# Q and K stacks written by DMAs inside SBUF instead of selection matmuls, in a gated cross-attention and mixture-of-experts block

## The reference

```python
x = x + tanh(g_xattn) * cross_attention(layernorm(x), ctx)   # softmax over 512 context rows
X = layernorm(x); h = rmsnorm(X) * norm1_w
q, k, v = h @ wq, h @ wk, h @ wv                             # 16 heads of 8
X = X + concat_heads(softmax(q k^T * 8**-0.5) v) @ wo        # 256 x 256 scores a head
h2 = rmsnorm(X) * norm2_w
combine = softmax weights of the top 2 of 8 experts (softmax(h2 @ router_w))
moe = swiglu_shared(h2) + sum_e combine[e] * swiglu_e(h2)    # inner width 256
x = x + tanh(g_ffn) * (X + moe)
```

## Time and profile before

| | us |
|---|---|
| median of three runs | 265.34 (265.28 to 267.71) |
| profiled execution | 265.57 |
| its span, first to last instruction | 263.8 |
| PE busy | 220.2 |
| DVE busy | 155.4 |
| ACT busy | 134.0 |
| POOL busy | 50.6 |

### The profile page before, as it was taken

One profiled execution on the slowest core, in us unless ns is written; L12 is line 12 of the kernel. 1 busy time (PEld: TensorE's weight loads), 2 busy tenths in 40 slices (PEclk: granted clock), 3 DMA queues, 4 the chain that ended last, 5 costly groups with the idle time before them and its releaser, 6 DMA issues.

```text
span 263.8 us, 4600 instructions
## 1 busy us (share of the span) xinstructions
PE 220.2 (83%) x1671; PEld 187.5 (71%) x1671; DVE 155.4 (59%) x397; ACT 134.0 (51%) x249; POOL 50.6 (19%) x81
## 2 busy tenths in 40 slices
PE   7791677787867788799979859999999959999995
PEld 6461556465756556577676639888899949999995
DVE  2658515880776935357438796663556565555554
ACT  2942364415286678698868744555424732222220
POOL 6609301154210700001810530011002000000000
PEclk9998668986799999999999998999999989999999
DMA  5900000002020210000330000000000000000000
GB/s 135 278 3 0 1 2 0 0 0 65 0 60 0 66 56 1 2 0 2 82 98 2 0 2 0 0 2 4 1 22 0 0 2 20 2 1 21 1 2 20
DMA packets 5174, 6.32 MB, mean 24 GB/s; under 512 B 448, under 2 KB 3392, under 8 KB 5152
## 3 DMA queue, kind: packets, MB, share of 16 engines
q1 hardware_dynamic: 5152, 6.02, 8.3%
HBM read 5.50 MB, written 0.52 MB: 23 GB/s over the span
## 4 chain that ended last, share of the span: by engine, by line
PE 58%; ACT 16%; DVE 15%; issue 6%; POOL 4%; DVEq 0%; ACTq 0%; POOLq 0%
PE bank L1051 11%; PE bank L1040 6%; PE bank L1039 6%; PE bank L1041 6%; PE bank L1022 5%; PE bank L1007 4%; ACT k_st L501 4%; PE bank L930 3%; PE bank L996 3%; DVE mxs L782 3%; ACT k_st L438 2%; ACT ep L548 2%; PE bank L1060 2%; PE bank L867 2%; PE bank L891 2%
## 5 line engine op out<-in xcount | busy, mean ns | idle before, releaser
L782 DVE TENSOR_REDUCE mxs<-bank 128x2 f32<-128x512 f32 x64 | 43.1, 689 | 20.4 <-PE bank L996 19.6
L548 ACT ACTIVATE ep<-bank 128x512 f32<-128x512 f32 x64 | 37.6, 599 | 19.3 <-PE bank L1007 18.2
L1039 PE MATMUL bank<-h2hi,whi 128*128 128x256 f32 x144 | 44.0, 306 | 0.0
L1051 PE MATMUL bank<-down_s,early 128*128 128x128 f32 x288 | 39.3, 280 | 3.4 <-DVE early L802 3.3
L1040 PE MATMUL bank<-h2lo,whi 128*128 128x256 f32 x144 | 41.4, 288 | 0.0
L1041 PE MATMUL bank<-h2hi,wlo 128*128 128x256 f32 x144 | 41.0, 285 | 0.0
L1051 PEld LDWEIGHTS bank<-down_s,early 128*128 128x128 f32 x288 | 36.1, 196 | 4.0 <-DVE early L802 4.0
L996 PE MATMUL bank<-k_st,q_st 96*128 96x256 f32 x128 | 30.8, 322 | 6.5 <-DVE mxs L782 3.8
L568 ACT ACTIVATE early<-bank 128x512 f32<-128x512 f32 x28 | 16.6, 597 | 38.2 <-PE bank L1041 38.2
L802 DVE TENSOR_TENSOR early<-early,bank 128x512 f32<-128x512 f32 x28 | 19.2, 687 | 27.9 <-PE bank L1041 21.4
L1007 PE MATMUL bank<-q_st,k_st 96*128 96x256 f32 x128 | 28.5, 304 | 2.7 <-ACT k_st L501 1.2
(11 more groups left out here) (146 smaller groups left out, 341.9 us busy)
## 6 DMA issues: line engine op xcount, KB each, us to landing
raw<-expert_w SPq DMA_DIRECT2D x9, 256.0 KB, 2.8
down_s<-expert_w SPq DMA_DIRECT2D x9, 128.0 KB, 2.7
early<-ctx_T SPq DMA_DIRECT2D x1, 672.0 KB, 9.3
xs<-x_tiles SPq DMA_DIRECT2D x2, 256.0 KB, 5.1
out_dram<-x SPq DMA_DIRECT2D x4, 128.0 KB, 2.0
ffn_s<-ffn_w SPq DMA_DIRECT2D x1, 261.0 KB, 9.3
attn_s<-attn_w SPq DMA_DIRECT2D x1, 242.0 KB, 2.8
early<-ctx_T SPq DMA_DIRECT2D x1, 224.0 KB, 6.4
```

The source lines that it names most:

```text
L548: nc.scalar.activation(ep[:, n % NEP].rearrange("p t s -> p (t s)"), b_of(("exp", n))[:], ACT.Exp, scale=SCALE_H).then_inc(free(("exp", n) ...
L782: nc.vector.tensor_reduce(mxs[:, half % 2, :, 64 + h:65 + h], b_of(("max", n))[:].rearrange("p (t s) -> p t s", t=TB), AX_X, ALU.max).then ...
L1039: pe.matmul(bank, whi[:, fs], h2hi[:, hs], start=True, stop=False)
L1051: last = pe.matmul(b_of(("down", n))[:, j * D:(j + 1) * D], act_t[:, n % 2, f * L + j * P:f * L + (j + 1) * P], down_s[:, f, e * D:(e + 1) ...
```

## The change

The stacks are written by DMAs from `split` to `q_st` and `k_st`, with no matmul or cast. `wq` and `wk` are reordered on the host (`by_parity`), so that one parity's heads are 64 neighbouring partitions; each DMA takes 64 partitions of 1 KB and writes eight partitions of 8 KB, 16 DMAs a sequence. SP issues them, but eight of sequence 0's are issued by ScalarE behind its `qk_split`. There are three stack buffers. Pads of buffer 0 are cleared by GpSimd early (step z), its picks are copied by ACT, and SP copies both to buffers 1 and 2 by eight DMAs (`copy_pads`). Rows beyond 64 are 16 instead of 32. For sequence 3, which takes buffer 0 again, GpSimd clears the maxima rows (step c3). Step t is GpSimd's clearing of `mxs` and `vh`, steps m its expert splits, now tied to the slots. `u`, `h2T`, `h2hi` and `h2lo` share memory with tiles that are no longer in use. Banks are given by kind from sets (`BANKS`), the one unused for longest first. All items up to the last slot use tanh.

```diff
-NSTACK = 2
+NSTACK = 3
-FIRST_STEPS = """f0 g0 xn0 f1 q0 g1 s0 xn1 s1 p0 q1 o0 p1 s2 o1 f2 s3 n0 p2 g2 h0 o2 xn2 p3 k0
-                 e0 q2 e1 o3 e2 w0 e3 n1""".split()
-MIXED_STEPS = {0: "s4 h1", 1: "f3", 2: "k1 s5", 3: "p4 g3", 4: "e4 xn3", 5: "o4 p5", 6: "e5 q3", 7: "o5 s6", 8: "e6 n2",
-               9: "p6 s7", 10: "e7 h2", 11: "o6", 12: "p7 k2", 13: "w1", 14: "o7", 16: "n3", 17: "e8", 19: "h3",
-               21: "e9 k3", 25: "e10", 29: "e11", 31: "w2", 33: "e12", 37: "e13", 41: "e14", 45: "e15", 47: "w3"}
+FIRST_STEPS = """f0 g0 xn0 f1 z0 q0 g1 s0 xn1 s1 p0 f2 q1 o0 p1 s2 g2 o1 s3 n0 p2 xn2 h0 o2 k0 p3 t0
+                 q2 o3 s4 n1 w0 f3 s5 h1 p4 k1""".split()
+MIXED_STEPS = {0: "g3 o4", 1: "p5 xn3", 2: "o5", 3: "q3 n2", 4: "s6", 5: "s7", 6: "h2", 7: "p6 w1", 8: "k2 o6 m0", 9: "p7",
+               10: "o7", 11: "n3 m1", 13: "h3", 15: "k3 m2 m3", 18: "m4", 27: "c3", 31: "w2", 42: "m5 m6 m7 m8", 47: "w3"}
+BANKS = {"turn": (0, 1, 6), "proj": (2, 3, 7), "sum": (4, 5), "misc": (4, 5)}
...
-    NSEL = 96
+    NSEL = 64 + NH
...
-    last_exp = NHEADS - 1 + LAG
+    last_exp = SLOTS_A
...
+        def stack(eng, b, heads):
+            s = b % NSTACK
+            eng.wait_ge(hi_ready, b + 1)
+            is_read(eng, ("qk2", b))
+            if b >= NSTACK:
+                is_full(eng, ("exp", NH * (b - NSTACK + 1) - 1))
+            for p in heads:
+                for a in range(2):
+                    for c in range(2):
+                        r = 32 * p + 16 * a + 8 * c
+                        for qk, part, stack in ((0, a, q_st[r:r + 8, s]), (1, c, k_st[r:r + 8, s, p * NG:(p + 1) * NG])):
+                            rows = split[64 * p:64 * p + 64, b % 2, part, qk, :].bitcast(F32)
+                            eng.dma_start(stack.bitcast(F32), rows).then_inc(stacked[b], 16)
+        def copy_pads(sp, s):
+            words, maxima = k_st[:].bitcast(F32), q_st[:].bitcast(F32)
+            sp.dma_start(words[0:32, s, NG:], words[0:32, 0, NG:]).then_inc(padded[s], 16)
+            sp.dma_start(words[32:64, s, :NG], words[32:64, 0, :NG]).then_inc(padded[s], 16)
+            sp.dma_start(words[64:NSEL, s], words[64:NSEL, 0]).then_inc(padded[s], 16)
+            sp.dma_start(maxima[64:NSEL, s], maxima[64:NSEL, 0]).then_inc(padded[s], 16)
...
-            for e in range(NEXP):
+            for e in range(NRAW):
+                load_expert(sp, e)
+            sp.wait_ge(picks_ready, 2)
+            sp.wait_ge(pads_ready, 1)
+            for b in range(1, NSTACK):
+                copy_pads(sp, b)
+            stack(sp, 0, (0,))
+            for b in range(1, NSTACK):
+                stack(sp, b, (0, 1))
+            for e in range(NRAW, 5):
+                load_expert(sp, e)
+            stack(sp, NSTACK, (0, 1))
+            for e in range(5, NEXP):
...
             def split_h2(b):
                 is_read(pool, ("h2T", b))
+                if b == 0:
+                    pool.wait_ge(stacked[2], 256)
+                    pool.wait_ge(stacked[3], 256)
...
                     qk_split(i)
                     if i == 0:
-                        copy_picks(1)
+                        stack(act, 0, (1,))
...
-                    if h % 4 == 0:
-                        written(("stq", n // 4))
-                        written(("stk", n // 4))
+                    if h == 0:
+                        if 1 <= b < NSTACK:
+                            pe.wait_ge(padded[b], 64)
+                        else:
+                            pe.wait_ge(pads_ready, b // NSTACK + 1)
+                        pe.wait_ge(stacked[b], 256)
```

More of the change, by code:

```diff
@@ L46, with bank_uses @@
 NRAW = 2
[L49 to L54, removed]
+def bank_uses(kinds, uses):
+    place, taken, count = {}, {}, {}
+    for n, (kind, use) in enumerate(uses):
+        bank = min(kinds[kind], key=lambda i: taken.get(i, i - 8))
+        place[use] = (bank, count.get(bank, 0))
+        taken[bank], count[bank] = n, count.get(bank, 0) + 1
     return place
@@ new lines, in _ @@
+            for stage, i in order:
+                if stage == "f":
+                    norm1(i)
+                elif stage == "g":
+                    if i == 0:
+                        pool.wait_ge(ld_attn, 16)
+                        pool.wait_ge(tg_ready, 1)
+                        step(nc.gpsimd.tensor_scalar(bv_row, bv_row, tg[:, 0:1], None, ALU.mult))
+                    add_bias(i)
+                elif stage == "o" and i % TB == TB - 1:
+                    norm2(i // TB)
+                elif stage == "z":
+                    pool.wait_ge(norm1_out, 2)
+                    pool.wait_ge(xb_ready, 1)
+                    clear_pads(i)
+                elif stage == "t":
+                    tables()
+                elif stage == "m":
+                    split_weights(i)
+                elif stage == "c":
+                    clear_maxima(i)
+                elif stage == "a":
+                    for kind, b in read_at.get(i, []):
+                        if kind == "square":
+                            norm3(b)
+                        if kind == "h2T":
+                            split_h2(b)
@@ L511, in misc @@
                     is_full(act, use)
-                    rows = b_of(use)[64:NSEL, 0:L].unsqueeze(1).broadcast_to([32, NG // 2, L])
+                    if b == 0 and half == 0:
+                        for i in range(1, NSTACK):
+                            act.wait_ge(padded[i], 64)
+                    rows = b_of(use)[64:NSEL, 0:L].unsqueeze(1).broadcast_to([NH, NG // 2, L])
                     nc.scalar.mul(q_st[64:NSEL, b % NSTACK, 4 * half:4 * half + 4, :], rows, -1.0).then_inc(free(use), 1)
@@ L833, in _ @@
                     qk_rest(i)
-                elif stage == "e" and i < 4:
-                    stack_out(i)
                 elif stage == "a":
@@ L918, in v2_proj @@
                 last.then_inc(full(("v2", b)), 1)
-            def make_stacks(i):
-                b, part = i // 4, i % 4
-                if i == 0:
-                    pe.wait_ge(sel_ready, 8)
-                pe.wait_ge(hi_ready, b + 1)
-                written(("qk2", b))
-                for qk, use, rows in ((0, ("stq", i), sel_q), (1, ("stk", i), sel_k)):
-                    may_fill(pe, use)
-                    for n in range(2):
-                        for hl in range(2):
-                            last = pe.matmul(b_of(use)[0:NSEL if qk == 0 else 64, n * L:(n + 1) * L],
-                                             rows[:, hl, 2 * part + n, :], split[:, b % 2, hl, qk, :],
-                                             start=(hl == 0), stop=(hl == 1))
-                    last.then_inc(full(use), 1)
             def misc(step, b):
@@ L1083, in _ @@
                     v2_proj(i)
-                elif stage == "e":
-                    make_stacks(i)
                 elif stage == "a":
```

153 lines of the change are left out of this document (43 added, 110 removed).

## The result

| | before | after |
|---|---|---|
| median us (runs) | 266.52 (4, same chip) | 247.30 (4; 245.17 to 248.91) |
| ratio, 95% interval | 1 | 0.925 [0.915, 0.935] |
| profiled execution, its span | 265.57, 263.8 | 245.17, 243.1 |

The account below looks back on a forecast made before the run. Steps waiting for each other at the start, no full engine, then PE with ACT, then DVE with PE, lastly PE bound it. Stages 45 + 31.5 + 36 + 24 + 99 = 235.5 us of span, forecast 237, range 222 to 256.

Parts of the forecast that it names:

- the forecast's own band of 230 to 245: Whole kernel: the time lands near the forecast of 237 us; chance 0.48.
- Slots 18 to 47: Third stage, stack groups between attention slots: their ACT and PE work goes, 36 us instead of 48.3, bounds 33 and 41.
- the rival of 252 (245 to 260): Between slots PE waits for DVE's maxima, not ACT's casts, so only PE's own share goes: 252 us; chance 0.25.
- The start: Everything ahead of slot 0: the later of ScalarE's path to k1 and the stack transfers, 45 us against 46.3, bounds 42 to 52.
- the narrow case: Stack transfers: eight of 64 written rows give an eighth of the ways, 1.87 us each, 30 us a sequence.
- Slots 0 to 17: Second stage: DVE's 26 us at its share of slots 48 to 63 give 31.5 us instead of 43.4, bounds 27 and 36.
- Transfers of sequences 1 to 3 hidden: Stack DMAs needed at slots 16, 32 and 48: at between 4 and 20 us a sequence no wait shows.
- The sign that I named: Stack DMAs: each lands under 10 us after its issue.
- the slower rival: Stack transfers become the bound, 30 us a sequence one after the other, slot 48 at 151, total 276 us; chance 0.07.
- Banks: PSUM: pv, down and small transposes share two banks instead of four; emptied in time, otherwise up to 12 us lost.
- Tail: Expert items behind slot 63: 99 us instead of 101.5, bounds 96 and 102; table loads cause part of five items' 5.9 lost.
- Expert loads and pad copies behind the stacks: SP's queue: expert loads behind stack DMAs have 16 slots of cover, and pad copies of 6.5 us run during the statistics.

Follow-up runs that it names:

- The copies and the matmuls put back: Two kernels: the changed kernel plus 24 ScalarE copies of 96x512, or plus eight more PE matmuls at each of eight slots from 17 to 45: 256.76 and 250.22 us.
- the y pairs free: Changed kernel with GpSimd waiting for DVE's norm pairs before clearing pads or tables and splitting experts 0 and 1: 236.51 us, 0.890 of before.
- the fastest kernel: Changed kernel with GpSimd waiting for DVE's norm pairs, stack rows four partitions apart, ScalarE's DMA issues behind its copy for p3: 230.36 us, 0.862 of before.

## Why the prediction came out as it did

The sign was right, and so was the mechanism of the large term. 247.3 lies in the range (222 to 256; the high ends had added up to 258), but not in the forecast's own band of 230 to 245. It lies in the band of a rival whose premise the runs refute. 237 was too low by 10. By its own steps:

*Slots 18 to 47* (36, measured 33.8). Right, and slightly too careful. The pace read from slots 48 to 62, 1.16 us, was the right row to read: measured 33.8 / 30 = 1.13. ACT's removed 13.9 us were 13.6 (38.34 to 24.73); PE's were 12.0 instead of 7 to 9. The copies and the matmuls put back showed that either engine's time counts, so that the rival of 252 (245 to 260), which the total alone would confirm, is refuted in its premise. ACT is at 73% of that stage, not below 70% as I wrote, since the stage itself is shorter.

*The start* (45, measured 48.8). Here the first mis-sized term is "SP's issues took 0.43 us each" for ScalarE's. They took 0.63 to 1.46, 6.6 us for eight where the sum had 3.4 (the bound of 7.8 held). The second is the 8 us behind them: from 37.3 to the end of k1's projection at 49.4 it took 12. I counted six further steps; the chain has fourteen short pieces on DVE alone, and two groups of matmuls of 2.1 us each at the lower clock (0.50). The third is the transfers: I took the value from 281 GB/s, a row of transfers spread over all partitions, and put the narrow case among the rivals. They took 17.9 us here and 18.4 to 18.7 later, between my ends of 4 and 30, near the 19 that the sentence on ports gave, and landed at 48.6 instead of 40.5. The 40.5 was itself no sum of its terms: 31 + 3.7 + 2.0 is 36.7, or 40.1 behind the last issue. Both paths were too short by 7 to 8 us, and slot 0 took the later of them. That the stage is only 3.8 us off is luck in part: 45 stood 2.5 us above the later of the two paths as summed. That is why undoing one of them alone measured nothing. The split came at 30.56, where I had 31.

*Slots 0 to 17* (31.5, measured 36.4, just over my bound of 36). The mis-sized term is the share of time in which DVE would be busy. DVE's work, put at 26, was 26.32; the 82% that I had read from slots 48 to 63 wasn't reached: 26.32 of 36.4 is 72%. With the y pairs free it was 72% again (23.54 of 32.5), and 75% in the fastest kernel (23.63 of 31.5). Slots 48 to 63 have no k steps, and these have: the views of waits for the stage, first before, then changed, show what DVE waited for at them (the first of the three waits, 4.0, began ahead of slot 0):

```profile
DVE split L686 <- ACT split L473: 2.3, 2, 1.5
```

```profile
DVE split L693 <- ACT split L500: 8.1, 3, 4.0
```

Which of these waits made the stage longer no run shows; the granted clock was 0.76 too, lower than the 0.88 of before. The expert splits m0 and m1 on the pairs of steps n2 and n3, which I had not seen, are not the step that failed: the kernel before had the same collisions, and the 28.75 us from which I took the 26 held them. That the fastest kernel needs 31.5 us, the number of the sum, is chance: less work of DVE at a lower share.

*Transfers of sequences 1 to 3 hidden.* Right: needed at slots 16, 32 and 48, and no wait there. The sign that I named, a landing under 10 us after its issue, came for the last transfers of sequences 1 to 3 (7.4 to 8.8 us) and not for sequence 0 (12). It was a poor sign: sixteen issues take 10.5 us themselves, which hides more than half of a slow transfer. With the slots where they were, transfers would have cost something beyond sequence 0 from some 26 us a sequence on (30.6 + 2 x 26 is 82.6, and slot 16 came at 82.1); the slower rival stayed off.

*Banks* (cover: each is emptied within a slot or two; up to 12 us lost). Nothing was lost. Fixed pairs are slower, by 4 us in slots 0 to 17.

*Tail* (99, measured 101.0). Too optimistic by 2. The mis-sized term is the part of the five items' 5.9 lost us that I gave to the table loads. With the silu and its loads put back the tail is 101.5. Most of what was lost there is one wait, 3.29 us of PE, that begins with ScalarE standing behind DVE's routing operations; the change took 0.9 us off it, with a table load gone, and left 2.37.

*Expert loads and pad copies behind the stacks* cost nothing visible. GpSimd's split of h2 waited 5.1 us for sequence 3's transfers, and item 0 did not wait in turn.

## What to carry to other kernels

Where two chains meet at one wait, an experiment that shortens one measures nothing; shorten both before you call either harmless. Ask of every DMA inside SBUF which partitions it writes, and spread the rows; ask also what stands behind the issues on the engine that issues them. Wherever GpSimd works in SBUF, look at what DVE does beside it, in the kernel that you start from too: four such pairs, slow in both kernels, were worth 8 to 9 us of the changed one, as much as a third of what the change was expected to bring. And take an engine's share of a stage from a stretch with the same steps in it.

## What the runs showed of the hardware

- Writing eight neighbouring partitions, 64 KB inside SBUF took 1.15 us from issue to landing (57 GB/s, sixteen in a row), a 1 KB packet 0.145 us at the median; with eight partitions four apart it was 0.046 us a packet, and sixteen transfers took 12.1 us, of which the issues took 10.5.
- Issuing such a DMA took SP 0.61 us (one each 0.655; 0.60 to 0.76 in sequence 0), ScalarE 1.46 for the first and 0.63 to 0.83 for the next seven, where SP's loads from HBM had taken 0.43.
- A GpSimd memset, which reads nothing, held a DVE pair as an operation with inputs did: 0.60 us alone, 1.97 to 2.18 beside one.
- The granted clock: with SP alone issuing, PE waited 8.65 us for DMAs, and from 38.9 to 56.0 the clock was at its lower level (0.50, 1.2 of 2.4 GHz). In the 6.9 us before it fell PE had been busy for 2.7. The first slots behind the wait ran at that level too.
